# Attention maxima carried in a spare row of the queries, and a reordered ScalarE list, in a fused decoder kernel

## The reference

```python
# 1: selective state-space mixer (256 channels, 16 states, conv of 4 taps)
h = layernorm(ln(x)) ; x_h, res = split(h @ W_in.T) ; x_h = silu(conv4(x_h))
dt, B, C = split(x_h @ W_x.T) ; dt = softplus(dt @ W_dt.T + b_dt)
s_t = exp(dt_t * A) * s_{t-1} + dt_t * B_t * x_t      # 256 channels x 16 states
y = sum_states(s * C) + x_h * D ; out = (y * silu(res)) @ W_out.T
# 2: cross attention, 16 heads of 8, 64 keys, masked softmax
score = q @ k.T / sqrt(8) ; score = where(mask == 0, -1e9, score)
x = x + softmax(score) @ v @ w_o + b_o
# 3: top-2 of 8 experts (128 -> 512 -> 128, relu), weighted by a softmax of the two gates
```

## Time and profile before

| | us |
|---|---|
| median of 3 executions | 828.37 |
| lowest, highest | 825.86, 828.56 |
| the profiled execution | 829.39 |
| its span | 827.6 |
| rounds (start of the first scan to the end of the last) | 31.24 to 604.24 |
| a whole round in the middle (copy of step 15 to copy of step 15) | 72.07 |

### The profile page before, as it was taken

One profiled execution on the slowest core, in us unless ns is written; L12 is line 12 of the kernel. 1 busy time (PEld: TensorE's weight loads), 2 busy tenths in 40 slices (PEclk: granted clock), 3 DMA queues, 4 the chain that ended last, 5 costly groups with the idle time before them and its releaser, 6 DMA issues. The chain is left out here.

```text
span 827.6 us, 12373 instructions
## 1 busy us (share of the span) xinstructions
PE 686.6 (83%) x3923; PEld 479.3 (58%) x3923; DVE 684.4 (83%) x1043; ACT 523.0 (63%) x1223; POOL 618.9 (75%) x467
## 2 busy tenths in 40 slices
PE   6578667988898988889888888876679889999993
PEld 3444324556465655546555555554457678899993
DVE  3579999999999999999999999999963564765674
ACT  4677747887976878797687879567133433333345
POOL 1177988977999998999999999999771334675553
PEclk9779878999999999999999999989799999999997
DMA  4534785554648555544753663387254324787765
GB/s 106 205 116 120 211 257 176 164 176 148 190 139 223 167 167 177 181 143 128 224 165 105 193 192 118 114 224 219 69 160 155 126 97 140 249 297 235 228 240 152
DMA packets 80411, 142.70 MB, mean 172 GB/s; under 512 B 10555, under 2 KB 53574, under 8 KB 80346
## 3 DMA queue, kind: packets, MB, share of 16 engines
q1 hardware_dynamic: 75802, 133.38, 52.1%
q0 software_dynamic: 4544, 8.54, 2.9%
HBM read 110.25 MB, written 37.27 MB: 178 GB/s over the span
## 5 line engine op out<-in xcount | busy, mean ns | idle before, releaser
L1526 POOL TENSOR_TENSOR prod<-hst,BC 128x1024 f32<-128x1024 f32 x128 | 301.2, 2361 | 52.9 <-DVE hst L1741 41.8
L1741 DVE TENSOR_TENSOR_SCAN hst<-dA,Rp 128x1024 f32<-128x1024 f32 x128 | 292.3, 2283 | 9.0 <-ACT dA L1222 0.4
L1222 ACT ACTIVATE dA<-dtm,Aneg 128x255 f32<-128x255 f32 x512 | 213.9, 495 | 52.9 <-DVE hst L1741 52.1
L1531 POOL TENSOR_TENSOR prod<-prod 128x512 f32<-128x512 f32 x128 | 161.2, 1270 | 2.4
L1732 DVE TENSOR_TENSOR Rp<-BC,Rp 128x1024 f32<-128x1024 f32 x128 | 156.9, 1226 | 6.0 <-DMA BC<-bcd 0.6
L655 PE MATMUL Y<-prod,ident 128*128 128x256 f32 x512 | 140.5, 407 | 18.1 <-POOL prod L1531 14.6
L1649 POOL DMA_INDIRECT y2d<-prod,back x78 | 77.2, 989 | 97.5 <-DVE prod L2118 80.7
L655 PEld LDWEIGHTS Y<-prod,ident 128*128 128x128 f32 x512 | 101.2, 205 | 55.4 <-POOL prod L1531 20.3
L655 PE MATMUL Mb<-hpad,winT 128*128 128x512 f32 (+1 forms) x176 | 82.2, 615 | 14.7 <-ACT xh L1171 10.4
L1570 POOL DMA_INDIRECT xsd<-x2o,slots x64 | 63.1, 986 | 17.5 <-issue 16.8
L655 PEld LDWEIGHTS Rp<-BC,xh 128*128 128x128 f32 x608 | 73.6, 192 | 3.6 <-issue 1.8
(11 more groups left out here) (289 smaller groups left out, 1134.9 us busy)
## 6 DMA issues: line engine op xcount, KB each, us to landing
BC<-bcd SPq DMA_DIRECT2D x63, 1024.0 KB, 5.6
BC<-recs SPq DMA_DIRECT2D x39, 578.0 KB, 4.0
xsd<-blank SPq DMA_DIRECT2D x17, 1056.0 KB, 11.8
dtm<-xsd SPq DMA_DIRECT2D x39, 132.0 KB, 4.0
recs<-in_L_ffn_W SPq DMA_DIRECT2D x16, 256.0 KB
xin<-in_x SPq DMA_DIRECT2D x8, 256.0 KB, 5.2
x2d<-x2o SPq DMA_DIRECT2D x8, 256.0 KB, 5.6
E<-x2d SPq DMA_DIRECT2D x4, 512.0 KB, 5.4
```

The lines of the kernel that those rows point to most:

```text
L1222: m = A(dA[:, k % RING, i, 1:SEQ], dtm[:, r % 2, d, b * SEQ + 1:(b + 1) * SEQ], ACT.Exp, scale=Aneg[:, d, c * NC + i:c * NC + i + 1])
L1526: TT(prod[:, k % RING, :, :], hst[:, k % RING, :, :], BC[:, (k // 2) % BCR, 1, :, :], ALU.mult).then_inc(s_pd, 1)
L1531: TT(prod[:, k % RING, 0:NC // 2, :], prod[:, k % RING, 0:NC // 2, :], prod[:, k % RING, NC // 2:NC, :], ALU.add).then_inc(s_fd, 1)
L1741: v.tensor_tensor_scan(hst[:, k % RING].rearrange("p n s -> p (n s)"), dA[:, k % RING].rearrange("p n s -> p (n s)"), U.rearrange("p n s - ...
```

## The change

Two things are changed together.

**The maxima.** `Kbd` gets a version for each w. Its keys are those of the heads of w, and in the rows that `qT[:, w]` leaves empty it has -1 in one row for each of the four key blocks (`kshift`). The maxima are turned as f32 and copied by ACT into those spare rows of `qT`, so that the matmul of the keys by the queries subtracts them itself. `split_max`, `nm`, `nmT`, `selmax` and their matmuls go. In `scores`, where no maxima are wanted yet, the spare rows still hold zeros. The mask in key order is turned once (`turn_mask`, `copy_mask`) and added by one bf16 matmul of 64 rows per quarter, in place of two of 128. `key_blocks` becomes eight instructions in place of four, with a bias column beside the scale column; `copy_max` becomes four of 32 rows in place of one of 96. `attention_scale` on DVE in round 0 gets six tiny instructions more.

**ACT's list.** `twice_contexts` moves from k = 5 to 3, `att_out` and `mixer_out` from 5 to 4, `copy_kv`, `att_square` and `key_blocks` from 6 to 5. At k = 6 `copy_xh(r, 1)` stands ahead of `spreads`, and the inverse root and one more `decays` ahead of the silus; from k = 7 to 12 `decays` run four ahead and at 13 none does. At k = 14 `inverse_roots_x` stands ahead of `copy_max`, and `copy_xh(r+1, 0)` follows it. Both first `exps` stand at k = 15. On PE `att_variance` moves ahead of `gate_in`.

```diff
-                        mm(T[h][:, w * SEQ:(w + 1) * SEQ], qT[rows, w, b, t * P:(t + 1) * P], Kbd[rows, b, :, :],
+                        mm(T[h][:, w * SEQ:(w + 1) * SEQ], qT[rows, 1 - w, b, t * P:(t + 1) * P], Kbd[rows, 1 - w, b, :, :],
...
             def turn_max(r):
-                pe.wait_ge(Tv.sem, Tv.at("me", r))
+                pe.wait_ge(Tv.sem, Tv.at("mx3b", r))
                 for i in range(NB * QT):
-                    m = pe.transpose(Tb[0:96, i * P:(i + 1) * P], nm[:, i, :, :], identb[:, :])
+                    m = pe.transpose(T[0][:, i * P:(i + 1) * P], mx[:, i, :], ident[:, :])
...
-                        o, hp = T[h][:, i * SEQ:(i + 1) * SEQ], TRIO[g][h][i]
-                        mm(o, selmax[:, hp, :], nmT[:, b * SEQ:(b + 1) * SEQ], start=False, stop=False, skip_group_check=True)
-                        for t in range(QT):
-                            m = mm(o[:, t * P:(t + 1) * P], mbias2[:, t, :, :], identb[:, :], start=False, stop=True,
-                                   skip_group_check=True)
+                        rows = slice(64 * h, 64 * h + 64)
+                        m = mm(T[h][:, i * SEQ:(i + 1) * SEQ], twice[rows, :, :], mbiasT[rows, :], start=False, stop=True,
+                               skip_group_check=True)
...
-                for j in range(HP // 2):
-                    m = A(Kbd[:, :, j, :], KT[:, :, :], ACT.Copy, scale=blk4[:, j:j + 1])
+                for w in range(2):
+                    for j in range(HP // 2):
+                        m = A(Kbd[:, w, :, j, :], KT[:, :, :], ACT.Identity, bias=kshift[:, w, j:j + 1], scale=kscale[:, w, j:j + 1])
...
-                A(nmT[:, :], Tb[0:96, 0:NB * SEQ], ACT.Copy).then_inc(Ta.sem, 1)
+                for w in range(2):
+                    for h in range(2):
+                        rows = slice(64 * h + 32 * (1 - w), 64 * h + 32 * (2 - w))
+                        m = A(qT[rows, w, :, :].rearrange("p b s -> p (b s)"), T[0][rows, :], ACT.Copy)
...
-                if prev and k == 5:
+                if prev and k == 3:
                     twice_contexts(r - 1)
-                if tail and k == 5:
+                if tail and k == 4:
                     att_out(r - 2)
                 if prev:
+                    if k == 4:
+                        mixer_out(r - 1)
                     if k == 5:
-                        mixer_out(r - 1)
-                    if k == 6:
                         copy_kv(r - 1)
+                        att_square(r - 1)
+                        key_blocks(r - 1)
+                if k == 6:
+                    copy_xh(r, 1)
                 if tail and k == 6:
                     spreads(r - 2)
...
-            def split_max(r):
...
-                if r and k == 14:
-                    v.wait_ge(Tv.sem, Tv.at("me", r - 1))
```

More of the change, by code:

```diff
@@ L328, in decoder @@
         Ta = Marks(sem("Ta"), "KT V sq ln rs q m e00 e01 e10 e11 ld rd x2")
-        Tv = Marks(sem("Tv"), "xq " + " ".join(f"mx{i}a mx{i}b" for i in range(NB * QT)) + " ma mb mc md me n")
+        Tv = Marks(sem("Tv"), "xq " + " ".join(f"mx{i}a mx{i}b" for i in range(NB * QT)) + " n")
         s_kb = sem("s_kb")
+        s_mk = sem("s_mk")
         s_cT = sem("s_cT")
@@ L913, in slot @@
                         steps_in(r + 1)
-                if prev and k == 5:
+                if prev and not nxt and k == 5:
                     att_variance(r - 1)
@@ L1000, in _, with turn_mask @@
             mm(T[0][:, SEQ:SEQ + 1], attT[:, 3, :], bv[:, :]).then_inc(s_tr, 1)
+            def turn_mask():
+                pe.wait_ge(s_k, 3)
+                pe.wait_ge(s_cT, 2)
+                for t in range(QT):
+                    m = pe.transpose(Tb[:, t * P:(t + 1) * P], mbias2[:, t, :, :], identb[:, :])
+                m.then_inc(s_mk, 1)
             def first_round(k):
@@ L1237, in copy_contexts, with copy_mask @@
                 A(cT[:, 4 * n:4 * n + 4, :], T[n][:, :].rearrange("p (r k) -> p r k", r=4), ACT.Copy).then_inc(s_cT, 1)
+            def copy_mask():
+                act.wait_ge(s_mk, 1)
+                A(mbiasT[:, :], Tb[:, 0:SEQ], ACT.Copy).then_inc(s_mk, 1)
             def twice_contexts(r):
@@ L1342, in slot @@
                     weight_sums(r - 2)
-                if prev and k == 5:
+                if prev and k == 3:
                     twice_contexts(r - 1)
-                if tail and k == 5:
+                if tail and k == 4:
                     att_out(r - 2)
                 if prev:
+                    if k == 4:
+                        mixer_out(r - 1)
                     if k == 5:
-                        mixer_out(r - 1)
-                    if k == 6:
                         copy_kv(r - 1)
+                        att_square(r - 1)
+                        key_blocks(r - 1)
+                if k == 6:
+                    copy_xh(r, 1)
                 if tail and k == 6:
                     spreads(r - 2)
-                if k == 6 and r < ROUNDS:
-                    copy_xh(r, 1)
                 if prev and k == 6:
-                    key_blocks(r - 1)
-                    att_square(r - 1)
+                    att_inverse_root(r - 1)
+                if k == 6:
+                    decays(r, 10)
                 if nxt and k == (6 if r else 7):
                     silus(r + 1)
-                if prev and k == 6:
-                    att_inverse_root(r - 1)
                 if tail and k == 7:
@@ L1373, in slot @@
                     square_x(r + 2)
+                if ln and k == 14:
+                    inverse_roots_x(r + 2)
                 if prev and k == 14:
                     copy_max(r - 1)
-                if ln and k == 14:
-                    inverse_roots_x(r + 2)
-                if prev and k >= 14:
-                    exps(r - 1, 0, k - 14)
+                if nxt and k == 14:
+                    copy_xh(r + 1, 0)
+                if prev and k == 15:
+                    exps(r - 1, 0, 0)
+                    exps(r - 1, 0, 1)
             def drain(r, k):
@@ L1446, in body @@
             def body(r, k):
-                g = r * STEPS + k + 3
-                if g < ROUNDS * STEPS:
+                g = r * STEPS + k + (4 if 7 <= k < 13 else 3)
+                if k != 13 and g < ROUNDS * STEPS:
                     decays(*divmod(g, STEPS))
-                if k == 15 and r + 1 < ROUNDS:
-                    copy_xh(r + 1, 0)
                 slot(r, k)
@@ L1889, in slot @@
                         maxima(r - 1, 3)
-                        split_max(r - 1)
                 if tail and k == 12:
@@ L1922, in drain @@
                         maxima(r - 1, k - 10)
-                    if k == 13:
-                        split_max(r - 1)
             v.wait_ge(s_first, FIRST)
@@ L1944, in _ @@
             nxt_(v.tensor_copy(identb[:, :], ident[:, :]))
-            nxt_(v.tensor_copy(selmax[:, :, :].rearrange("p g (h k) -> p (g h) k", h=2), pickmax[:, :].unsqueeze(2).to_broadcast([96, HEADS, KEYS])))
+            for h in range(2):
+                half = slice(64 * h, 64 * h + 64)
+                nxt_(v.tensor_copy(twice[half, :, :], ident[half, half].unsqueeze(1).to_broadcast([64, 2, KEYS])))
             v.wait_ge(s_prea, 1)
```

57 lines of the change are left out of this document (28 added, 29 removed).

## The result

The changed kernel takes 850.69 us (median of 4, 849.22 to 852.55) where the kernel before took 828.2 in the same comparison: a ratio of 1.0279, 95% interval 1.0246 to 1.0312. That is 22.5 us slower; the forecast was 16.5. The profiled execution has a span of 850.0 against 827.6. The last scan ends at 626.48 against 604.24, and from there to the end are 223.5 us against 223.4. So all of the loss lies in the rounds.

What follows compares the result with a forecast made beforehand. DVE was taken to set the pace up to about 604 us, with PE behind. -7.9 (split_max) + 28.5 (stalls less rstdt waits) - 4.1 (drain) = +16.5 us on the median 828.37, so 845; range 832 to 855.

Steps and rivals of the forecast that it cites:

- rival B: PE's gate waits lower its clock; 1 to 2.5 us more in each of rounds 2 to 6: 850 to 858, chance 0.07.
- split_max goes: On DVE's path, 1.31 us less a round; 7.9 us less over rounds 1 to 6.
- ACT's list ahead of spreads: In rounds 2 to 7, work ahead of spreads makes DVE's least wait 5.2 or 4.3 us, together 29.4 more.
- through PE's list, whose order is unchanged: Between DVE's normalise and the centring: a DVE faster elsewhere shifts both ends alike, so nothing earlier moves the chain.
- So I count no second wait: At select and the first maxima, each 5.2 later: ACT and PE arrive with about 1 us to spare.
- Decays ... costs nothing: On ACT, the decays now behind x1T fit in front of the keys at no cost.
- 29.4 - 0.9 - 5 x 1.31: Rounds 2 to 7: 29.4 us of stalls, less DVE's rstdt waits of 0.9 and split_max of 1.31 a round.
- Round 1 has no tail, so it has no such wait: In round 1, no stall at least of the 5.2 or 4.3 us counted for rounds 2 to 7.
- inside rounds both are hidden: Four copies (1.6 us more) and f32 turns (0.2 more) cost nothing in rounds; four later steps precede DVE's need.
- The drain, -4.1 with two split_max: Last two attentions: shorter quarters 5.1 us less, two split_max 2.6 less, copies and turns 3.6 more; net 4.1 less.
- -12 on the maxima and +28.5 on the order: Maxima: 7.9 us less in rounds and 4.1 less in the drain; order: 29.4 of stalls less 0.9 of rstdt waits.
- the 0.43 that was taken: On PE, four bf16 matmuls of 256 columns stay in a quarter, 0.43 us where 1.07 was; 0.64 less a quarter.

Runs made afterwards that it cites:

- e3: The changed kernel with key_blocks moved from ahead of copy_xh and spreads to behind spreads; 849.21 us, ratio 1.0237.
- e5: The changed kernel with one group of decays moved from behind x1T to between x2o and x1T on ACT; 849.33 us, ratio 1.0255.
- e1: The change's maxima alone, with ACT's and PE's order of the kernel before; 856.13 us, ratio 1.0340 to the kernel before.
- e7: e1 plus the change's order on ACT for the end of a round (steps from 9 on), the middle as before; 834.18 us, ratio 1.0092.
- e6: The changed kernel with, in the expert part, PE's first quarter of second scores behind the next tile_down; 849.66 us, ratio 1.0256.
- e7b: The program of e7 measured once more, without a change; 834.25 us, ratio 1.0069.

## Why the prediction was right, and where not

The range and the sign held, and so did the chain it was built on; its rival B held as well, since 850.69 lies at the lower edge of B's 850 to 858 and B's sign, a wait at `select`, is in the trace. Step by step:

- **split_max goes, -1.31 a round.** Right as far as DVE goes: the rows are gone, and a round without waits is 70.0 us.
- **ACT's list ahead of spreads.** The durations held, the stall less so. From the start of `normalise` to the end of POOL's pair were 15.96 us (262.63 to 278.59); now they are 19.99. The weak step is "through PE's list, whose order is unchanged": its order is, but its time is not. From `normalise` to the end of the centring were 12.0 in round 3 and are 10.9 now, so the stall was 4.2, shared by the copy of x and `least`, where 5.2 was forecast. `att_out`, before and then after:

```profile
263.35 0.49 PE L655 MATMUL T<-attT,oT 128*128 128x128 f32 x2 [2.01 <-DVE oT L1779]
...
264.04 0.63 PE L655 MATMUL T<-attT,oT 128*128 128x128 f32 x2
```
```profile
268.90 0.38 PE L655 MATMUL T<-attT,oT 128*128 128x128 f32 x2
```

  Before, PE had stood still for 2.01 and these matmuls ran at the lower level in part (granted clock 0.86 from 263 to 275 us); now it comes from the convolution without idle time and has 1.00 (267.5 to 279). That holds for rounds 2 to 4. In rounds 5 and 6 the stretch took 10.4 before and takes 10.9 now, and their stall of 4.2 is close to the 4.3 forecast.
- **"So I count no second wait".** Wrong by about 1.0 in five rounds, at `select`. This is rival B at its lower end, and what B gives as its mechanism is in the rows: PE waits 5.97 at the gates and the gates take 3.61. No run holds the clock up with the waits in place, so B's share apart from the load on ACT is not shown. ACT's waits for the gates are 14.8 us in the rounds where they were 5.4. Beyond that, e3 shows the error in kind: the stall at `least` was priced as an end in itself, while the same load is asked for again at `select`. Taking it from one place moved it to the other.
- **"Decays ... costs nothing".** Right, and e5 shows why: ACT waits for PE's keys anyhow.
- **Rounds 2 to 7 together.** +20.5 measured. The forecast's terms for them are 29.4 - 0.9 - 5 x 1.31 = +21.9, of which `split_max` of round 7 (counted in the drain) takes another 1.3: +20.6. The misses cancel: the copy of x and `least` waited 25.8 in place of 29.4, `select` 5.1 in place of 0, and the wait at the gate logits, on which the sum is silent, fell from 2.0 to 0.4.
- **Round 1.** Forecast -1.3, measured +2.1. "Round 1 has no tail, so it has no such wait" is true of `least`, but the step looked at no other wait. There the root, now ahead of the silus, waits 2.97 for PE, which is behind with eight matmuls of 5.75, and DVE waits 3.2 at its gating multiply.
- **copy_max, "inside rounds both are hidden".** True of the changed kernel, false of the maxima by themselves: e1 pays 18.3 for it. The prediction gave the order at the end of a round no value at all; e7 puts it at 22 us. It was the part of the order that paid.
- **The drain, -4.1 with two split_max.** Nothing came. The quarters are shorter as forecast: start to start 1.29 (692.80 to 694.09) against 1.98 (669.62 to 671.60) in the kernel before, 0.69 less where 0.64 was taken. In the last attention the price of the longer `copy_max` and the turns, 1.8, was right: PE waits 2.48 for it against 0.68. What the sum left out is the group behind it, which then runs below the full level (granted clock 0.67 from 692.8 to 698.0), 1.5 more; e6 takes 2.6 of the two back. And of the attention before it almost nothing came, though all four of its quarters were counted: from its turn to the first product with the values were 15.97 us (597.01 to 612.98) and are 15.71 (619.38 to 635.09). PE waits for ACT's exponentials, 1.17 each, ahead of most of these quarters, and after the change two of them (622.51 and 625.95 us) have their scores at the lower level for part or all of the time, 1.84 and 2.08 where others take 1.14; before it was one.
- **Additivity.** The sum put -12 on the maxima and +28.5 on the order, with the longer key blocks (1.9 a round) counted under the order. The runs say +28 for the maxima alone, +27 for the order alone, and +22.5 for both. That the total came near is partly luck.

The Trainium skill, "ScalarE: Activation LUTs" ("What ACT_TABLE_LOAD costs"), gave 2.4 us for four copies by columns alone, an estimate; the trace has 2.38, and 587 ns for one of 32 rows. By the Trainium skill, "TensorE: Matmul & The Clock Gate" (Part 3, packing small matmuls), the bf16 part of a quarter would have been 0.2, an estimate, on two halves of the rows at once; the rows have 0.32 for four (693.77 to 694.09), between that and the 0.43 that was taken.

## What to carry to other kernels

A list that runs without idle time has several places where another engine comes for its results. Price a move at the last of them, not only at the next: what leaves the path to one turns up at the next unless it leaves the list. Before summing the parts of a change, ask which part pays for which: here the order at the end of a round, which the sum had at nothing, held 22 us. And look for work that hangs on nothing late, such as keys made from fixed contexts, and put it where the list already waits.

## What the runs showed of the hardware

- An ACT copy of 32 rows by 512 columns takes 587 ns in the kernel after, one of 96 rows by 512 took 593: fewer rows save nothing here, so splitting by rows multiplies the time.
- TensorE's granted clock differed between executions of one program. The same four matmuls took 1.99 after 2.44 us of standing still and 3.78 after 3.36, but also 1.98 after 3.48 and 3.46 after 2.41 (e7 and e7b), and whole executions lay at 826.55 and at 831 to 838. After waits of 5 us and more they took 3.4 to 3.8 in every trace here.
- A bias column beside the scale column (and `Identity` in place of `Copy`) costs ACT 0.08 us on 128 columns: eight took 3.18, four without it 1.26.
